# Perceiver block on one core: key chunks drawn over a block boundary, and the state space's small matmuls in pairs

## The chip, the cores and the metric
One NeuronCore of one Trainium2 chip runs the whole program. The metric is the device time of one execution in microseconds (us). TensorE (PE) does the matmuls, VectorE (DVE), ScalarE (ACT) and GpSimd (POOL) the elementwise work, SyncE (SP) issues most DMAs. Every engine runs its own list of instructions in order; semaphores tie the lists together.

## The reference, cut to what matters
One transformer-like block on x (8 x 64 x 512), in float32, three parts with a residual each.

```python
# 1. cross attention: q from x, k and v from ctx (8 batches x 1601 keys), 32 query heads, 8 key heads, head size 128
q = rmsnorm(layernorm(x) @ Wq.T);  k = rmsnorm(ctx @ Wk.T);  v = ctx @ Wv.T
x = x + softmax(q @ k.T / sqrt(128)) @ v @ Wo.T
# 2. state space (Mamba-2 form): 64 heads of 64, 8 groups of state size 128, causal convolution of 4 taps
gate, hbc, dt = split(layernorm(x) @ Win)
xs, B, C = split(silu(conv(hbc)));  dt = softplus(dt + bias)
state = state * exp(-dt * A) + dt * xs outer B;  y = state . C + D * xs      # over 64 tokens
y = y * rsqrt(mean(y * y) per group + eps) * norm_weight * silu(gate)
x = x + y @ Wout
# 3. routed low-rank experts: 8 experts, rank 16, the best one per token
x = x + experts(x)
```

All large products are computed as three float16 matmuls: each operand is split into a high and a low half (high x high, high x low, low x high). ScalarE makes the high half, VectorE or GpSimd the low one.

## The kernel before, in words
The program is a chain of blocks: `queries`, `cross_attention`, `output_projection`, `state_space_and_experts`. A block begins on all engines together, once all have ended the one before.

`queries` (L910) makes the queries of 32 heads in 8 groups of 4 tiles. TensorE projects a tile into one of four PSUM banks `pQ`, and two tiles later (`LAG = 2`) turns the normed tile with four transposes into one of two banks `pR` (`turn`, L1059 on), from which ScalarE (`high`) and VectorE (`low`) make the two halves. `turn` of tile n waits for VectorE's low half of tile n - 2. In gaps the block also splits the key and value weights and the context of batch 0. After the loop TensorE has the last two `turn`s; SyncE stores the last group to DRAM and ends the block.

`cross_attention` (L51) works through 64 units (8 batches x 8 key heads). "Fills" (projections of keys, 4 chunks of 400 or 401 columns, and of values, tiles in pairs) go through three PSUM banks `pF`: fill n waits for `fill_lo >= n - 2`, that is, until VectorE has taken the low half of fill n - 3. Around the change:
- Ahead of the first unit TensorE does four key fills, three value fills, `squares(0, 0)` (norms of the keys, by ones columns) and `turn_squares(0, 0)`. ScalarE copies the squares (`gather_squares`), VectorE adds eps (`norms`), GpSimd raises to -1/2 (`power`), and with that VectorE can evict scores (`evacuate`). VectorE's 12 memsets of constants come first in its list; ScalarE, GpSimd and SyncE (mask loads, then query loads) wait for `consts >= 5`.
- A unit on TensorE: seven score pieces with key fills of the next unit between them, one value fill (`vals(0)`), the values of the unit before, the transposes of the maxima, the next unit's squares, the spreading of the maxima, `vals(1)`, `turn_squares`. VectorE evicts scores in seven pieces, takes the maximum (one instruction of 6 us), and then the low halves of key chunks 2 and 3 (`keys(2)`, `keys(3)`).

`state_space_and_experts` (L1452) works through 8 groups g, software-pipelined by a list written out by hand for each engine: `body(g)` for g = 0 to 6 and `last` for g = 7; `on(f, g, lag, ...)` calls f for group g - lag. Per group TensorE has ten input chunks (`input_chunk`, 12 matmuls each, round three banks `pI`), four output tiles (`out_tile`, 12 matmuls each, all in bank `pO`, so that each waits for VectorE's `accumulate` of the one before), and for each of four token tiles the small float32 pieces:
- `turn_x` (L1738, transposes into the X half of the two banks `ab`), read by VectorE's `times_dt`;
- `keys_by_queries` (L1749, into `cd`), read by `causal`;
- `decay` (L1707, into the D half of `ab`, of GpSimd's `ramp`), read by ScalarE's `exponentials`;
- `outputs` (L1724, into `cd`), needs VectorE's `masked` and `times_dt`, read by `skip_added`;
- `squares` (L1757, into `cd`).
A piece waits for the readers of what was begun in its banks (the `begun` counts). Large matmuls are all at L797, the helper `split3`. VectorE's and ScalarE's `split_B`, `split_A` and `split_C` make the halves of the gate columns, the other input columns and the output weights of a group; `gates` (ScalarE) evicts the first four input chunks, `taps` and `finish_conv` do the convolution of the other six.

Of the kernel before, what the change touches and what calls it, by code (L numbers as in the profile page):

```python
# [10 lines left out]
P = 128  # L11
BATCH, TOK, HID = 8, 64, 512
KEYS = 1601
# [37 lines left out]
def cross_attention(nc, ctxT, maskT, kv_parts, ctx_parts, q_hi, q_lo, q_stored, o_dram, out_proj, NB=BATCH):  # L51

    with ExitStack() as ctx:
# [52 lines left out]
        proj = sem("proj")  # L106
# [152 lines left out]
        def _(pe):  # L259
# [98 lines left out]
            for i in range(NCH):  # L358
                key_fill(i, i, 0, 0, 0, i)
            for f in range(3):  # L360
                value_fill(NCH + f, NCH + f, 0, 0, f)
            pe.wait_ge(consts, 5)
            pe.wait_ge(idt, 2)
            squares(0, 0)
            turn_squares(0, 0)

            def body(b, par):
                for s in range(U):
# [55 lines left out]
                    vals(1)  # L424
# [13 lines left out]
        def _(act):  # L438
# [109 lines left out]
        def _(dve):  # L548
            dve.memset(k_h[:, :, KEYS:KPAD], 0.0)
            dve.memset(k_l[:, :, KEYS:KPAD], 0.0)  # L550
            dve.memset(sq_h[:, KEYS:KPAD], 0.0)
            dve.memset(sq_l[:, KEYS:KPAD], 0.0)
            dve.memset(pick[:, :, :], 0.0).then_inc(consts, 1)
            dve.wait_ge(consts, 1)
            for j in range(4):
                dve.memset(pick[:, j, j:j + 1], 1.0)
            dve.memset(half[:, :], -0.5)
            dve.memset(lnb[:, :], P_LN)
            dve.memset(ones_h[:, :], 1.0).then_inc(consts, 1)
            dve.memset(mask[:, KT - 1, :], NEG).then_inc(consts, 1)  # L560
            dve.memset(v_h[:, :, KT - 1, :], 0.0).then_inc(consts, 1)
            dve.memset(v_l[:, :, KT - 1, :], 0.0).then_inc(consts, 1)

# [94 lines left out]
            for i in range(NCH):  # L658
                key_fill(i, i, 0, i)
            for f in range(3):  # L660
                value_fill(NCH + f, NCH + f, 0, f)
            dve.wait_ge(mask_in, 32)

            def body(b, par):
                last = is_last(b)
                for s in range(U):
# [13 lines left out]
                    norms(b, s)  # L680
# [49 lines left out]
        def _(pool):  # L730
# [15 lines left out]
            pool.wait_ge(consts, 5)  # L746
            for i in range(NCH):
                low_squares(i, 0, 0, i)

# [160 lines left out]
def queries(nc, x, wqT, norm_w, q_hi, q_lo, kvT, ctxT, kv_parts, ctx_parts, stored):  # L910
# [4 lines left out]
    with ExitStack() as ctx:  # L915
# [36 lines left out]
        pT = [ctx.enter_context(nc.psum_tensor(f"q_pT{i}", [P, 512], F32)) for i in range(2)]  # L952
        pQ = [ctx.enter_context(nc.psum_tensor(f"q_pQ{i}", [P, 512], F32)) for i in range(TT)]
# [102 lines left out]
        def _(pe):  # L1056
# [28 lines left out]
            for t in range(TT - LAG, TT):  # L1085
                turn(GR // 2 - 1, 1, t)
# [365 lines left out]
def state_space_and_experts(nc, start, winG, woutG, params, x1, raT, bwT, out):  # L1452

    with ExitStack() as ctx:
# [125 lines left out]
        def _(pool):  # L1580
# [29 lines left out]
            def body(g, par):  # L1610
                on(join_squares, g, 2, 3)
# [3 lines left out]
                on(low, g, 2, 3)  # L1615
                on(ramp, g, 0, 0)
                on(low, g, 1, 0)
                on(join_squares, g, 1, 0)
                on(ramp, g, 0, 1)
                on(join_squares, g, 1, 1)  # L1620
                on(low, g, 1, 1)
                on(join_squares, g, 1, 2)
                on(low, g, 1, 2)
            def last(g, par):

                ramp(g - 1, 2)
                join_squares(g - 2, 3)
                low(g - 2, 3)
                power(g - 2)
                join_squares(g - 1, 0)  # L1630
                low(g - 1, 0)
                join_squares(g - 1, 1)
                ramp(g - 1, 3)
                ramp(g, 0)
                join_squares(g - 1, 2)
                low(g - 1, 1)
                join_squares(g - 1, 3)
                ramp(g, 1)
                low(g - 1, 2)
# [19 lines left out]
        def _(pe):  # L1659
# [7 lines left out]
            def input_chunk(g, n):  # L1667
# [4 lines left out]
                if n == GCH:  # L1672
                    wait(pe, wA_lo, g + 1)
                if n >= 3 + GCH:
# [786 lines left out]
```

## Time and profile before

| | |
|---|---|
| median of 3 runs | 2343.58 us (2342.84 to 2344.61) |
| profiled execution | 2342.31 us, span 2340.3 us |
| mean granted TensorE clock | 0.992 of full speed |
| PE | 2285.0 us busy, 98% of the span |
| DVE | 1917.5 us, 82% |
| ACT | 1297.5 us, 55% |
| POOL | 1579.3 us, 67% |
| queries end, attention begins | 118.5 us |
| state space begins | 1928.5 us |

Busy time is the union of an engine's instructions. The engines overlap, so the shares don't add up; the work of an engine that nothing waits for costs nothing. Times in the rows below are us from the span's start.

### The profile page before, as it was taken

What the parts mean: (1) busy time and instruction counts of PE and PEld (TensorE: products, weight loads), DVE (VectorE), ACT (ScalarE), POOL (GpSimd) and SP (SyncE); (2) the same over time, 40 slices, a digit from 0 to 9 for tenths busy, and PEclk for the clock granted to TensorE, in tenths of its full rate; (3) what the DMA queues carried; (4) which work ended last, traced back from release to release, by engine and by line L of the source; (5) the groups of instructions that cost most, each with busy time, mean ns of one, the idle gap of its engine ahead of it and who ended that gap; (6) DMA issues with size and microseconds to landing.
All of it is one profiled execution on the core that took longest, in us unless ns stands there. A gap on an engine that the chain in (4) does not pass through costs nothing. (4 is left out here: it accounts for less than half of the span.)

```text
span 2340.3 us, 46521 instructions
## 1 busy us (share of the span) xinstructions
PE 2285.0 (98%) x19276; PEld 1647.7 (70%) x19276; DVE 1917.5 (82%) x2600; ACT 1297.5 (55%) x2091; POOL 1579.3 (67%) x1059
## 2 busy tenths in 40 slices
PE   8999999999999999999999999999999898999998
PEld 4567787777877778777787777877778444445544
DVE  7858888888888888888888888888879957888877
ACT  7845455554555545555455555555545536666664
POOL 0138888888878888888887888888888402344432
PEclk9999999999999999999999999999999998999999
DMA  8421100000100011001000110100001443212210
GB/s 290 126 53 29 29 23 26 27 28 24 29 26 23 29 27 34 18 26 28 27 26 26 31 28 18 34 26 10 12 26 59 146 149 108 82 64 82 91 46 19
DMA packets 101166, 117.54 MB, mean 50 GB/s; under 512 B 8286, under 2 KB 70878, under 8 KB 100958
## 3 DMA queue, kind: packets, MB, share of 16 engines
q1 hardware_dynamic: 98942, 107.25, 14.5%
q0 software_dynamic: 2016, 7.34, 1.2%
q8 instruction: 153, 2.51, 0.5%
q14 instruction: 55, 0.45, 0.1%
HBM read 96.74 MB, written 17.83 MB: 49 GB/s over the span
## 5 line engine op out<-in xcount | busy, mean ns | idle before, releaser
L176 POOL TENSOR_TENSOR p_l<-S,p_h 128x1792 f16<-128x1792 f32 x126 | 423.6, 3362 | 204.8 <-ACT p_h L483 204.8
L598 DVE SCALAR_TENSOR_TENSOR S<-pS,rk,mask 128x256 f32<-128x256 f32 x832 | 355.5, 478 | 131.7 <-PE pS L263 84.9
L263 PE MATMUL p_acc<-w_l,ctx_h 128*128 128x256 f16 (+1 forms) x1664 | 453.6, 273 | 0.0
L263 PE MATMUL p_acc<-w_h,ctx_l 128*128 128x256 f16 (+1 forms) x1664 | 453.6, 273 | 0.0
L263 PE MATMUL p_acc<-w_h,ctx_h 128*128 128x256 f16 (+1 forms) x1664 | 453.6, 273 | 0.0
L608 DVE TENSOR_REDUCE mx<-S 128x256 f32<-128x3328 f32 x63 | 376.6, 5979 | 2.2
L263 PE MATMUL p_acc<-ctx_h,w_h 128*128 128x400 f16 (+1 forms) x1024 | 341.5, 334 | 3.0 <-PEq L915 3.0
L263 PE MATMUL p_acc<-ctx_l,w_h 128*128 128x400 f16 (+1 forms) x1024 | 341.5, 334 | 0.0
L263 PE MATMUL p_acc<-ctx_h,w_l 128*128 128x400 f16 (+1 forms) x1024 | 340.7, 333 | 0.0
L465 ACT ACTIVATE v_h<-p_acc 128x512 f16<-128x512 f32 (+1 forms) x224 | 126.7, 566 | 376.2 <-PE p_acc L263 376.2
L645 DVE TENSOR_TENSOR S<-S,pO 128x1792 f32<-128x1792 f32 (+1 forms) x128 | 240.9, 1883 | 86.3 <-PE pO L333 86.3
L737 POOL TENSOR_TENSOR sq_l<-sq_f,sq_h 128x400 f16<-128x400 f32 (+1 forms) x256 | 242.5, 947 | 71.3 <-ACT sq_h L457 71.3
L263 PE MATMUL pS<-qh,k_h 128*128 128x256 f16 x832 | 226.6, 272 | 1.8 <-DVE S L598 1.8
L263 PE MATMUL pO<-p_h,v_h 128*128 128x256 f16 x832 | 226.8, 273 | 0.0
L263 PE MATMUL pO<-p_l,v_h 128*128 128x256 f16 x832 | 226.8, 273 | 0.0
L263 PE MATMUL pO<-p_h,v_l 128*128 128x256 f16 x832 | 226.8, 273 | 0.0
L263 PE MATMUL pS<-qh,k_l 128*128 128x256 f16 x832 | 226.8, 273 | 0.0
L263 PE MATMUL pS<-ql,k_h 128*128 128x256 f16 x832 | 226.7, 272 | 0.0
L476 ACT ACTIVATE S<-S,lnb 128x1792 f32<-128x1792 f32 (+1 forms) x128 | 215.5, 1683 | 15.3 <-DVE S L645 15.3
L184 POOL TENSOR_TENSOR S<-S 128x1536 f32<-128x1536 f32 x63 | 216.8, 3441 | 0.1
L453 ACT ACTIVATE k_h<-p_acc 128x400 f16<-128x400 f32 (+1 forms) x256 | 129.6, 506 | 148.6 <-PE p_acc L263 146.6
L483 ACT ACTIVATE p_h<-S 128x1792 f16<-128x1792 f32 (+1 forms) x128 | 203.7, 1591 | 0.3
(285 smaller groups left out, 5221.9 us busy)
## 6 DMA issues: line engine op xcount, KB each, us to landing
ctx_p<-ctxT_dram SPq DMA_DIRECT2D x42, 458.0 KB, 3.6
s_wst<-winG_dram SPq DMA_DIRECT2D x8, 1536.0 KB, 6.5
q_wst<-wqT_dram SPq DMA_DIRECT2D x8, 1024.0 KB, 6.5
o_scratch<-o_st SPq DMA_DIRECT2D x32, 256.0 KB, 2.4
s_wst<-winG_dram SPq DMA_DIRECT2D x8, 1024.0 KB, 5.3
m_wost<-woutG_dram SPq DMA_DIRECT2D x8, 1024.0 KB, 5.2
qh<-q_hi_scratch SPq DMA_DIRECT2D x64, 64.0 KB, 1.9
ql<-q_lo_scratch SPq DMA_DIRECT2D x64, 64.0 KB, 2.0
```

Source lines behind the costliest of these rows:

```text
L176: eng.tensor_tensor(p_l[:, s % 2, t0:t1, :], S[:, s % 2, t0:t1, :], p_h[:, s % 2, t0:t1, :], ALU.subtract).then_inc(pl_ok, 1)
L184: eng.tensor_tensor(T[:, 0:6, :], T[:, 0:6, :], T[:, 6:12, :], ALU.add).then_inc(sum_ok, 1)
L263: mm = pe.matmul(out, x, y, start=first and j == 0, stop=final and j == 2)
L453: act.activation(k_h[:, head % 2, c0:c0 + w], bank[:, 0:w], ACT.Copy, scale=S_KV / (S_CTX * S_W))
L465: act.activation(v_h[0:m, job % 2, 2 * f:2 * f + tiles, :], pF[at % 3][0:m, 0:256 * tiles].rearrange("p (t c) -> p t c", c=256), ACT.Copy, ...
L476: act.activation(S[:, s % 2, t0:t1, :], S[:, s % 2, t0:t1, :], ACT.Exp, bias=lnb[:, 0:1]).then_inc(ph_ok, 1)
L483: act.activation(p_h[:, s % 2, t0:t1, :], S[:, s % 2, t0:t1, :], ACT.Copy).then_inc(ph_ok, 1)
L598: ins = dve.scalar_tensor_tensor(out=S[:, s % 2, t, :].rearrange("p (r q) -> p r q", r=REP), in0=bank[:, t % 2, :].rearrange("p (r q) -> p ...
L608: dve.tensor_reduce(mx[:, :], S[:, s % 2, :, :].rearrange("p t q -> p q t"), AX.X, ALU.max).then_inc(mx_ok, 1)
L645: dve.tensor_tensor(v, v, pO[s % 2][:, 1, :].unsqueeze(1).to_broadcast([P, t1 - t0, QC]), ALU.subtract).then_inc(sub_ok, 1)
L737: pool.tensor_tensor(sq_l[:, c0:c0 + w], sq_f[:, c0:c0 + w], sq_h[:, c0:c0 + w], ALU.subtract).then_inc(sql_ok, 1)
```

## The change
Two things. In `queries` and `cross_attention`: the four banks of the output projection (`fills`) are now shared by `queries`, the semaphore `proj` lives in both blocks, and the first two key fills of unit 0 are issued by TensorE at the end of `queries`, each behind one of the last two `turn`s. `cross_attention` starts with fill 2; squares and their transpose are put between the value fills, VectorE makes its constants behind two key chunks, and in the first unit `vals(1)` stands ahead of `turn_maxima`. In the state space: all four hand-written lists are reordered, and output tile 1 of groups 0 to 5 goes to bank `pI[1]`, with the waits for it.

```diff
 queries, TensorE
-            for t in range(TT - LAG, TT):
-                turn(GR // 2 - 1, 1, t)
+            def first_keys(i):
+                c0, w = CH[i]
+                wait(pe, kv_lo, 1)
+                wait(pe, ctx_lo, i + 1)
+                for k in range(KC):
+                    mm = split3(pe, fills[i][:, 0:w], (kv_h[:, 0, k, 0:HD], kv_l[:, 0, k, 0:HD]),
+                                (ctx_h[:, k, c0:c0 + w], ctx_l[:, k, c0:c0 + w]), k == 0, k == KC - 1)
+                mm.then_inc(proj, 1)
+            for i in range(AHEAD):
+                turn(GR // 2 - 1, 1, TT - LAG + i)
+                first_keys(i)
 cross_attention, TensorE ahead of the units
-            for i in range(NCH):
+            for i in range(AHEAD, NCH):
                 key_fill(i, i, 0, 0, 0, i)
-            for f in range(3):
-                value_fill(NCH + f, NCH + f, 0, 0, f)
+            value_fill(NCH, NCH, 0, 0, 0)
             pe.wait_ge(consts, 5)
             pe.wait_ge(idt, 2)
             squares(0, 0)
+            value_fill(NCH + 1, NCH + 1, 0, 0, 1)
             turn_squares(0, 0)
+            value_fill(NCH + 2, NCH + 2, 0, 0, 2)
 in a unit
                     if earlier:
                         values(*earlier, 0)
+                    else:
+                        vals(1)
                     if ahead:
                         turn_maxima(b, s)
 ...
                     spread_maxima(b, s)
-                    vals(1)
+                    if earlier:
+                        vals(1)
 ScalarE
-            act.wait_ge(consts, 5)
             for i in range(NCH):
                 key_fill(i, i, 0, 0, i)
-            for f in range(3):
+            value_fill(NCH, NCH, 0, 0, 0)
+            gather_squares(0, 0)
+            act.wait_ge(consts, 5)
+            for f in range(1, 3):
                 value_fill(NCH + f, NCH + f, 0, 0, f)
-            gather_squares(0, 0)
 VectorE (the memsets were the first thing in its list; norms(0, 0) was in the first unit)
-            for i in range(NCH):
+            key_fill(0, 0, 0, 0)
+            key_fill(1, 1, 0, 1)
+            constants()
+            for i in range(2, NCH):
                 key_fill(i, i, 0, i)
-            for f in range(3):
+            value_fill(NCH, NCH, 0, 0)
+            norms(0, 0)
+            for f in range(1, 3):
                 value_fill(NCH + f, NCH + f, 0, f)
 state space, waits on TensorE
+                if n == 1:
+                    wait(pe, acc, TT * (g - 1) + 2)
 ...
                 if bank is pO:
-                    wait(pe, acc, TT * (g + 1) + t)
+                    wait(pe, acc, TT * (g + 1) + (1 if t == 2 and g < L - 1 else t))
+                elif g < L:
+                    wait(pe, conv, CONV * (g + 1) + GCH)
 TensorE's body, as it was and as it is
-  input_chunk 0 | turn_x(g-1,3) | out_tile(g-2,3) | decay(g-1,3) outputs(g-1,2) | input_chunk 1, 2 |
-  squares(g-1,0) keys_by_queries(g-1,3) | input_chunk 3 | decay(g,0) outputs(g-1,3) | input_chunk 4 to 7 |
-  squares(g-1,1) | input_chunk 8, 9 | squares(g-1,2) squares(g-1,3) turn_x(g,0) | out_tile(g-1,0) |
-  keys_by_queries(g,0) turn_x(g,1) keys_by_queries(g,1) decay(g,1) | out_tile(g-1,1) |
-  decay(g,2) outputs(g,0) | out_tile(g-1,2) | keys_by_queries(g,2) turn_x(g,2) outputs(g,1)
+  input_chunk 0 | turn_x(g-1,2) keys_by_queries(g-1,1) | out_tile(g-2,3) | decay(g-1,2) outputs(g-1,1) |
+  input_chunk 1 | squares(g-1,0) turn_x(g-1,3) keys_by_queries(g-1,2) | input_chunk 2 |
+  decay(g-1,3) outputs(g-1,2) | input_chunk 3 | squares(g-1,1) keys_by_queries(g-1,3) | input_chunk 4 |
+  decay(g,0) outputs(g-1,3) | input_chunk 5 to 9 | squares(g-1,2) squares(g-1,3) turn_x(g,0) |
+  out_tile(g-1,0) | out_tile(g-1,1) in pI[1] | turn_x(g,1) keys_by_queries(g,0) | out_tile(g-1,2) |
+  decay(g,1) outputs(g,0)
 VectorE's body begins
-  split_B(g), accumulate(g-2,1), skip_added(g-1,0), masked(g-1,1), causal(g-1,2), gated(g-1,0), ...
+  split_B(g), times_dt(g-1,1), causal(g-1,0), masked(g-1,0), accumulate(g-2,1), accumulate(g-2,2),
+  skip_added(g-1,0), gated(g-1,0), times_dt(g-1,2), causal(g-1,1), masked(g-1,1), split_A(g), ...
 and ends (before)  taps(g,5), times_dt(g,0), accumulate(g-1,0), causal(g,0), times_dt(g,1), causal(g,1), masked(g,0)
 and ends (now)     taps(g,5), times_dt(g,0), accumulate(g-1,0)
```

ScalarE's list has both splits before the second exponentials, then square and high half of each tile in turn, and the gates in two runs of two; `split_C` on VectorE is cut in two halves; GpSimd joins the squares and makes the low half of a tile right after each other. `last` follows the same order up to input chunk 5.

## Rows read from the trace of the kernel before

**Rows 1.** Windows: start:end and length, busy us (instructions) by engine, granted clock, DMA.
```profile
118.50:124.40 5.90, 5.87 (x19) 2.66 (x20) 1.72 (x16) 1.29 (x3) 0.65 (x3) 0.51 0.96 238
160.00:200.00 40.00, 40.00 (x344) 31.41 (x342) 31.84 (x47) 25.56 (x36) 30.23 (x18) 1.00 0.10 27
2060.93:2107.57 46.64, 45.72 (x386) 23.45 (x386) 38.90 (x61) 31.52 (x41) 18.81 (x18) 1.00 0.24 80
```
**Rows 2.** Timeline of TensorE at the seam: start, duration, instruction, idle before it.
```profile
111.52 1.04 PE L1066 MATMUL q_pR<-q_ident,q_qs 128*128 128x128 f32 x8
114.93 0.63 PE L1066 MATMUL q_pR<-q_ident,q_qs 128*128 128x128 f32 x4 [2.38 <-DVE q_ql L1177]
118.53 0.49 PE L263 MATMUL p_acc<-ctx_h,w_h 128*128 128x400 f16 x1 [2.97 <-PEq L915]
...
127.42 0.33 PE L263 MATMUL p_acc<-ctx_h,w_h 128*128 128x401 f16 x1
...
129.46 0.27 PE L263 MATMUL p_acc<-w_h,ctx_h 128*128 128x256 f16 x1
```
**Rows 3.** Timeline of SyncE's DMA queue, the last issue of the queries' block.
```profile
117.51 0.58 SPq L1008 DMA_DIRECT2D q_lo_scratch<-q_ql  x1
```
**Rows 4.** Timeline of TensorE, its waits in the first unit of the attention.
```profile
138.40 0.33 PE L318 MATMUL p_acc<-ident,zr 128*128 128x128 f32 x1 [0.37 <-ACT zr L471]
...
142.54 0.28 PE L263 MATMUL pS<-qh,k_h 128*128 128x256 f16 x1 [0.47 <-DVE S L598]
...
156.33 0.44 PE L326 MATMUL pO<-ident,mx 128*128 128x128 f32 x2 [1.82 <-DVE mx L608]
```
**Rows 5.** Timeline of VectorE, low halves of key chunks 2 and 3 behind the maximum.
```profile
156.18 1.06 DVE L573 SCALAR_TENSOR_TENSOR k_l<-p_acc,k_h 128x400 f16<-128x400 f32 x2
```
**Rows 6.** Timeline of TensorE, four stops of a steady state-space group.
```profile
2100.45 0.38 PE L797 MATMUL m_b<-m_woh,m_yl 128*128 128x512 f16 x1
2101.24 0.45 PE L1749 MATMUL m_cd<-m_bc 128*64 128x64 f32 x8 [0.41 <-ACT m_bc L1955]
2101.62 0.66 PE L1738 MATMUL m_ab<-s_ident,m_xq 128*128 128x128 f32 x4
2102.21 0.45 PE L1749 MATMUL m_cd<-m_bc 128*64 128x64 f32 x8
2103.16 0.66 PE L1707 MATMUL m_ab<-m_R,s_after 64*64 64x256 f32 x8 [0.49 <-DVE m_dtx L2179]
2103.75 0.39 PE L797 MATMUL m_b<-m_woh,m_yh 128*128 128x512 f16 x1
...
2106.14 0.38 PE L797 MATMUL m_b<-m_woh,m_yl 128*128 128x512 f16 x1
...
2107.51 0.39 PE L797 MATMUL m_b<-m_woh,m_yh 128*128 128x512 f16 x1
...
2109.89 0.38 PE L797 MATMUL m_b<-m_woh,m_yl 128*128 128x512 f16 x1
...
2111.88 0.39 PE L797 MATMUL m_b<-s_th,s_wh 128*128 128x512 f16 x1
...
2114.26 0.38 PE L797 MATMUL m_b<-s_th,s_wl 128*128 128x512 f16 x1
...
2114.91 0.38 PE L797 MATMUL m_b<-m_woh,m_yh 128*128 128x512 f16 x1
```
**Rows 7.** Timeline of ScalarE, its split of the gate columns.
```profile
2101.09 1.90 ACT L1925 ACTIVATE s_wh<-s_wst 128x2048 f16<-128x2048 f32 x1
```
**Rows 8.** Timeline of VectorE, from the second product to its split of the gate columns.
```profile
2102.32 0.69 DVE L2179 TENSOR_TENSOR m_dtx<-m_ab,m_dtq 128x512 f32<-128x512 f32 x1 [0.29 <-PE m_ab L1738]
...
2103.72 2.29 DVE L2120 SCALAR_TENSOR_TENSOR s_wl<-s_wst,s_wh 128x2048 f16<-128x2048 f32 x1
```
**Rows 9.** Timeline of GpSimd, two ramps.
```profile
2103.92 2.99 POOL L1585 TENSOR_TENSOR m_R<-m_upto,m_a 128x512 f32<-128x512 f32 x1 [4.83 <-PE m_ab L1707]
...
2108.00 1.04 POOL L1585 TENSOR_TENSOR m_R<-m_upto,m_a 128x512 f32<-128x512 f32 x1
```

More of the change, by code:

```diff
@@ L548, in _ @@
         def _(dve):
[L549 to L562, printed above, removed]
             def ctx_split(b, par, n):
@@ L656, in output, with constants @@
                                          op0=ALU.mult, op1=ALU.mult).then_inc(o_ok, 1)
-            for i in range(NCH):
+            def constants():
+                dve.memset(k_h[:, :, KEYS:KPAD], 0.0)
+                dve.memset(k_l[:, :, KEYS:KPAD], 0.0)
+                dve.memset(sq_h[:, KEYS:KPAD], 0.0)
+                dve.memset(sq_l[:, KEYS:KPAD], 0.0)
+                dve.memset(pick[:, :, :], 0.0).then_inc(consts, 1)
+                dve.wait_ge(consts, 1)
+                for j in range(4):
+                    dve.memset(pick[:, j, j:j + 1], 1.0)
+                dve.memset(half[:, :], -0.5)
+                dve.memset(lnb[:, :], P_LN)
+                dve.memset(ones_h[:, :], 1.0).then_inc(consts, 1)
+                dve.memset(mask[:, KT - 1, :], NEG).then_inc(consts, 1)
+                dve.memset(v_h[:, :, KT - 1, :], 0.0).then_inc(consts, 1)
+                dve.memset(v_l[:, :, KT - 1, :], 0.0).then_inc(consts, 1)
+            key_fill(0, 0, 0, 0)
+            key_fill(1, 1, 0, 1)
+            constants()
+            for i in range(2, NCH):
                 key_fill(i, i, 0, i)
-            for f in range(3):
+            value_fill(NCH, NCH, 0, 0)
+            norms(0, 0)
+            for f in range(1, 3):
                 value_fill(NCH + f, NCH + f, 0, f)
@@ L678, in vals_earlier @@
                             value_fill(FILLS * eb + slot(es, NCH + i), slot(es, NCH + i), job, f)
-                    norms(b, s)
+                    if earlier:
+                        norms(b, s)
                     vals_earlier(0)
@@ L907, in identity, with queries @@
                        pattern=[[-1, P]], channel_multiplier=1).then_inc(sem, 1)
-def queries(nc, x, wqT, norm_w, q_hi, q_lo, kvT, ctxT, kv_parts, ctx_parts, stored):
+def queries(nc, x, wqT, norm_w, q_hi, q_lo, kvT, ctxT, kv_parts, ctx_parts, stored, fills, proj):
     with ExitStack() as ctx:
@@ L951, in queries @@
         ql = sb("q_ql", [P, 2, BATCH, 4 * TOK], F16)
-        pT = [ctx.enter_context(nc.psum_tensor(f"q_pT{i}", [P, 512], F32)) for i in range(2)]
-        pQ = [ctx.enter_context(nc.psum_tensor(f"q_pQ{i}", [P, 512], F32)) for i in range(TT)]
+        pT = fills[0:2]
+        pQ = fills[2:4] + [ctx.enter_context(nc.psum_tensor(f"q_pQ{i}", [P, 512], F32)) for i in range(2, TT)]
         pR = [ctx.enter_context(nc.psum_tensor(f"q_pR{i}", [P, 512], F32)) for i in range(2)]
@@ L2019, in body @@
                 on(first_tap, g, 0, 2)
+                on(high, g, 1, 3)
                 on(finish_conv, g, 0, 1)
@@ L2346, in last @@
                 tile_mean_square(g, 0)
-                split_C(g, par)
+                split_C(g, par, range(GCH))
                 skip_added(g, 1)
```

199 lines of the change are left out of this document (100 added, 99 removed).

## The prediction
> **What bounds the kernel now.** I read the windows first, then TensorE's own order of instructions, then the engines that feed it. In the attention TensorE has no idle time (40.00 us busy of 40); in a steady group of the state space it is busy 45.72 of 46.64 us, with VectorE at 38.90, ScalarE at 31.52 and GpSimd at 18.81 [rows 1]. So a change pays only where it shortens TensorE's own list or fills one of its few holes. The reader is to look at two places. One is the seam between the queries and the attention, where TensorE stands still and then runs at half clock. The other is what lies between two runs of large state-space matmuls (168 a group, one each 0.216 us): the stops for small matmuls, waits included.
>
> **The seam.** The last query chunk runs straight into two sets of transposes, from 111.52; the last set runs at 114.93, after 2.38 us of waiting for the low half of an earlier tile; then nothing until the attention's block opens at 118.53 [rows 2]. SyncE's last store issue ends at 118.09 [rows 3], so that one sets the opening, and the change leaves it alone. From 118.50 to 124.40 the granted clock is 0.51, the 1.2 GHz level, behind 6 us in which the engine did next to nothing; in the later stretch it is 1.00, 2.4 GHz [rows 1].
> The change puts key chunk 0 between those transposes and key chunk 1 behind them. A chunk at the full clock takes 129.46 - 127.42 = 2.04 us [rows 2]. Chunk 0 runs from about 112.6 to 114.6, before the 114.93 at which the next transposes could start anyway; chunk 1 from 115.6 to 117.6, before 118.09. Both are free.
> (1) Before, the four chunks take from 118.53 to 129.46, 10.93 us. Afterwards two stand behind the opening, 4.1 us if the clock holds: 6.9 us gained. I take it to hold, since TensorE's holes shrink from 2.4 and 3.0 us to about 0.3 and 0.9. Bounds: if the clock falls all the same, 5.9 us of matmuls behind the opening run at half rate and 2.95 us of the 6.9 are lost; nothing in the list can gain more than 6.9.
> (2) VectorE's and GpSimd's work behind the three value fills is drawn between them. Before, TensorE waits 0.37 us for ScalarE's copy of the squared norms, and 0.47 us at 142.54 for score evictions that start late because GpSimd's power comes late [rows 4]. In the new order norms and power run under the third value fill (24 matmuls, 2.6 us), so both waits go: 0.8 us; bounds 0 and 0.84.
> What could be late there: the constants stand behind two key chunks on VectorE, about 3 us later than now, and SyncE's mask loads and behind them the query loads wait for them. The first scores come at 118.5 + 4.1 + 3 x 2.6 + 0.8 = 131.2 and I see these loads landed by 129; if not, the mask holds VectorE for a microsecond. The value fill into bank 1 needs VectorE's low half of chunk 1, ready about 121.7, wanted at 122.6.
> (3) In the first unit the second value fill now goes ahead of the transposes of the maxima, into a hole of 1.82 us [rows 4]. I give it nothing. The fill reuses one of three banks and waits for the low half of key chunk 2 of this unit, which VectorE does only behind that same maximum. So the hole stays and gets longer by this low half: two of them take 1.06 us [rows 5], so 0.5 us is lost; bounds -1.0 and, if I misread the order, +1.8.
> Sum at the seam: 6.9 + 0.8 - 0.5 = 7.2 us.
>
> **The state space.** No large matmul is added or removed, so I price stops. In one group, with the last large matmul's 0.216 us taken off [rows 6]:
> - keys, transposes, keys, decay: 2100.45 to 2103.75, 3.08 us, of which 0.41 waits for ScalarE's last convolution, 0.49 for VectorE's product, and about 0.2 for the first keys' eviction.
> - decay, outputs: 2106.14 to 2107.51, 1.15 us.
> - keys, transposes, outputs: 2109.89 to 2111.88, 1.77 us.
> - transposes alone: 2114.26 to 2114.91, 0.43 us.
> The other stops of a group (squares, and the rest of decay with outputs) cost the same in both orders. The new order turns the first, third and fourth of these into three pairs of transposes and keys and one more pair of decay and outputs; no two pieces of a pair write one bank, so neither waits for VectorE to have read the other's. Transposes and keys as a pair are not in the trace. Keys take 0.38 where nothing holds the next piece (2101.24 to 2101.62), so the pair can't be under 0.43 + 0.38 = 0.81; from above, transposes to keys at 0.59 (2101.62 to 2102.21) with keys at 0.38 behind gives 0.97, and some tenths for a drain 1.07. I take 0.90, nearer the unhindered row. So before 3.08 + 1.77 + 0.43 = 5.28, after 3 x 0.90 + 1.15 = 3.85: 1.43 us a group, bounds 0.9 and 1.7. The period goes from 46.64 to 45.2.
> Are the waits really covered? I set the end of output tile 0 (2100.45 + 0.22) at 0. ScalarE's split of the gate columns starts at 0.42 and takes 1.90 [rows 7]; VectorE's half of it (2.29) follows, and now stands ahead of the second product, the causal product and the first masked product, which take 1.40 in all (2102.32 to 2103.72) [rows 8]. The split ends at 4.6, the product at 5.3, the masked one at 6.0. TensorE goes through tile 1, a pair and tile 2 (2.59 + 0.90 + 2.59) and reaches the second decay at 6.1, which needs the product, and the outputs about 6.6, which need the masked one: 0.6 us to spare, the tightest place, and the whole next group is queued behind it. The second output tile, now in input bank 1, finds its convolution done; the next chunk 1 into that bank comes at 14.4, and the accumulation that frees it ends near 6.7. The gate that frees bank 0 for chunk 3 now stands behind VectorE's other split and ScalarE's second high half; by the same durations it ends at 20, wanted at 21.7. The convolutions follow their input chunks by about 1 us, as before.
> Five intervals between steady groups and the last group, taken as one more, give 6 x 1.43 = 8.6. The step from group 0 to group 1 has no output tiles to cover anything and pays latency in either order; I take 0.5 us for it, bounds one group's gain either way.
> Sum: 9.1 us, bounds 6 x 0.9 - 1.4 = 4.0 and 6 x 1.7 + 1.4 = 11.6.
>
> **Total.** 7.2 + 9.1 = 16.3 us. The profiled execution has a span of 2340.3 and takes 2342.31; it would take 2326.0. The median of the runs is 1.27 us above it, so the forecast is 2327.3.
>
> **Rivals.**
> A. The clock falls at the seam all the same. For it: TensorE still pauses twice around the opening. Against it: 4 of the 6 quiet microseconds are filled. Price 2.95: 2330.2. The Trainium skill ("TensorE: Matmul & The Clock Gate", Part 1, What's actually happening) says that a restart costs a stretch of time and not a number of matmuls; by that rule the two chunks that leave the half-clock stretch would only be replaced in it by those that follow, and the result is this rival's. The trace shows one such stretch here and can't yet tell.
> B. The state space gains nothing, because a covered wait comes back elsewhere. For it: the 0.6 us above. Against it: VectorE keeps 6 us free in a group. Only the seam is left: 2336.4.
> C. Slower than before. One mechanism: VectorE's split of the gate columns, now ahead of the three products, meets GpSimd's ramp, and both stretch. The ramp takes 2.99 us beside that split and 1.04 elsewhere [rows 9]. The outputs wait from the point at which that chain is 0.6 us late, and each microsecond beyond is paid in 7 groups. To eat 7.2 and 9.1 it would have to be 0.6 + 16.3/7 = 2.9 us late in each; at 4 us late the time is 2343.6 - 16.3 + 7 x 3.4 = 2351.1. Against it: the split is at 2.29 with the ramp already beside it, so the stretch falls on GpSimd, which has time. The Trainium skill ("GPSIMD Engine Reference", 1. Specifications) says that GpSimd shares its SBUF interfaces with VectorE, with contention when VectorE's instruction has two SBUF inputs; by it a new order can add such meetings. The ramp's two durations agree.
> D. The pair costs 0.81 and the step out of group 0 gains as a full group: 6 x 1.7 + 1.4, so 2.5 more: 2324.8.
>
> **Chances.** Forecast as told 0.50, A 0.17, B 0.13, D 0.13, C 0.04, and 0.03 for no change by some mix of these. Range 2321.5 to 2337.5: it holds A, B and D with a microsecond or three of margin. What a measurement of this kernel can't tell from no change is 0.2%, 4.7 us. Faster by more than that 0.92, within it 0.04, slower 0.04.
>
> **What would show it.** At the seam: key matmuls between 112.6 and 117.6, the attention's first matmul still at 118.5, a granted clock near 1 from there to 124, first scores near 131.2, and a TensorE wait of about 2.4 us ahead of the first unit's second value fill. In the state space: a period of 45.2, transposes and keys at 0.90, no wait of the decay for VectorE and none of the keys for ScalarE. A period of 46.6 with new TensorE waits for the masked product would make B or C right; an opening of the block later than 118.5 would break the seam's sum.

## The result and the profile after

| | before | changed |
|---|---|---|
| median (range) | 2344.10 us (2342.64 to 2345.77, 6 runs) | 2327.75 us (2326.76 to 2329.58, 6 runs) |
| profiled execution, span | 2342.31, 2340.3 us | 2328.39, 2326.0 us |
| mean granted clock | 0.992 | 0.994 |

The ratio is 0.9929, with a 95% interval of 0.9919 to 0.9939: faster by 16.4 us. The forecast was 2327.3.

To see where the time went I cut the two profiled executions at the same instructions: the start of the last query matmul, the first scores of the first and of the second attention unit, the first matmul of the state space, the end of each group's last input chunk, and the end of the span.

| stretch, us | before | changed | difference | forecast |
|---|---|---|---|---|
| last query matmul to first scores | 27.26 | 19.92 | -7.34 | -7.3 |
| first scores to the second unit's | 22.05 | 21.58 | -0.47 | 0.0 |
| from there to the state space | 1767.94 | 1767.94 | 0 | 0 |
| its start to group 0's last chunk | 30.23 | 30.19 | 0 | 0 |
| step from group 0 to 1 | 45.18 | 45.57 | +0.4 | -0.5 |
| five steady groups | 5 x 46.64 | 5 x 45.30 | -6.7 | -7.2 |
| step from group 6 to 7 | 49.28 | 47.60 | -1.68 | -1.4 |
| from there to the end | 53.86 | 55.35 | +1.49 | 0 |

Windows of the changed kernel (start:end and length, then busy us and instructions by engine, granted clock, DMA), answering to [rows 1]: queries' end, the attention's opening, a steady group, and a stop near the end with what follows it.
```profile
112.44:118.58 6.14, 4.85 (x31) 2.66 (x28) 2.94 (x5) 2.63 (x9) 0.04 (x1) 1.00 0.54 156
118.58:124.40 5.82, 5.82 (x41) 3.90 (x42) 3.21 (x19) 4.95 (x12) 3.46 (x6) 1.00 0.58 162
1996.55:2041.85 45.30, 45.30 (x386) 23.52 (x385) 39.62 (x62) 32.07 (x40) 16.81 (x17) 1.00 0.25 82
2270.65:2274.55 3.90, 1.74 (x15) 1.24 (x14) 2.68 (x5) 3.66 (x4) 2.03 (x2) 0.88 0.01 2
2274.55:2277.10 2.55, 2.55 (x8) 0.90 (x7) 1.53 (x3) 2.43 (x4) 0.00 (x0) 0.51 0.00 0
```
The opening runs 41 matmuls at a granted clock of 1.00 where 19 ran at 0.51 [rows 1]. The group is 1.34 us shorter, and TensorE has no idle time left in it. Near the end the clock falls, which the kernel before doesn't show in its 3.49 us stop at this place:
```profile
2286.44:2289.93 3.49, 1.33 (x15) 0.88 (x14) 2.27 (x5) 3.24 (x4) 2.03 (x2) 1.00 0.01 2
2289.93:2292.50 2.57, 2.57 (x14) 1.08 (x11) 1.95 (x3) 2.46 (x4) 0.00 (x0) 1.00 0.00 0
```
TensorE at the seam in the changed kernel, answering to [rows 2] (start, duration, instruction, idle before it and its releaser):
```profile
111.56 1.04 PE L1080 MATMUL q_pR<-q_ident,q_qs 128*128 128x128 f32 x8
112.44 0.33 PE L811 MATMUL p_acc<-ctx_h,w_h 128*128 128x400 f16 x1
...
114.98 0.63 PE L1080 MATMUL q_pR<-q_ident,q_qs 128*128 128x128 f32 x4 [0.35 <-DVE q_ql L1203]
115.44 0.33 PE L811 MATMUL p_acc<-ctx_h,w_h 128*128 128x400 f16 x1
...
117.31 0.33 PE L811 MATMUL p_acc<-ctx_h,w_l 128*128 128x400 f16 x1
118.58 0.33 PE L265 MATMUL p_acc<-ctx_h,w_h 128*128 128x400 f16 x1 [0.94 <-PEq L929]
...
148.75 0.28 PE L265 MATMUL p_acc<-w_h,ctx_h 128*128 128x256 f16 x1 [2.31 <-DVE k_l L565]
```
Both chunks lie in the old holes, and the opening hasn't moved. The last row is the first unit's second value fill, waiting for the low half of key chunk 2. Neither wait of 0.37 nor of 0.47 [rows 4] is in the trace any more.

A steady group's stops in the changed kernel, answering to [rows 6]. Between the rows run large matmuls, 12 or 24 at a time; L1767 turns, L1778 are the keys, L1736 the decay, L1753 the outputs, L1786 the squares:
```profile
2047.86 0.60 PE L1767 MATMUL m_ab<-s_ident,m_xq 128*128 128x128 f32 x4
2048.39 0.45 PE L1778 MATMUL m_cd<-m_bc 128*64 128x64 f32 x8
2051.47 0.66 PE L1736 MATMUL m_ab<-m_R,s_after 64*64 64x256 f32 x8
2051.95 0.64 PE L1753 MATMUL m_cd<-m_E,m_dtx 64*64 64x64 f32 x32
...
2062.40 0.28 PE L1786 MATMUL m_cd<-s_ones,m_sqb 128*128 128x1 f32 x2
2062.54 0.64 PE L1767 MATMUL m_ab<-s_ident,m_xq 128*128 128x128 f32 x4
2063.10 0.45 PE L1778 MATMUL m_cd<-m_bc 128*64 128x64 f32 x8
```
No row has a wait. From the end of the last large matmul to the start of the next, the pair is 0.91 us twice and 1.09 with the squares in it; decay and outputs stay at 1.15.

### The profile page after: what moved, and what is told of

Its sections match the earlier page's. It is cut to its first block and busy times, and to the rows that moved or that the text cites. A ratio compares the mean times of both kernels' runs of the same rounds, so it can differ in the third digit from the quotient of the medians.

```text
span 2326.0 us, 46522 instructions
## 1 busy us (share of the span) xinstructions
PE 2278.8 (98%) x19276; PEld 1646.9 (71%) x19276; DVE 1920.4 (83%) x2600; ACT 1301.6 (56%) x2091; POOL 1569.2 (67%) x1059
## 3 DMA queue, kind: packets, MB, share of 16 engines
q0 software_dynamic: 2016, 7.34, 1.2%
## 5 line engine op out<-in xcount | busy, mean ns | idle before, releaser
L265 PE MATMUL p_acc<-ctx_h,w_h 128*128 128x400 f16 x1016 | 337.6, 332 | 0.9 <-PEq L929 0.9
L265 PE MATMUL p_acc<-ctx_l,w_h 128*128 128x400 f16 x1016 | 337.6, 332 | 0.0
L265 PE MATMUL p_acc<-ctx_h,w_l 128*128 128x400 f16 x1016 | 336.9, 332 | 0.0
```

The costliest lines, as they stand in the source:

```text
L265: mm = pe.matmul(out, x, y, start=first and j == 0, stop=final and j == 2)
```

## The experiments
Twelve kernels, each timed in five rounds (state_only has seven times). A ratio is against the kernel before on the same chip, whose medians there were 2344.1 to 2345.3 us, so medians of different rows can differ by about a microsecond for the chip alone. The columns are stretches of one profiled execution, as in the table above: A last query matmul to the second unit's first scores, B step 0 to 1, C one steady group, D step 6 to 7 and the rest to the end.

| kernel | median | ratio (interval) | A | B | C | D |
|---|---|---|---|---|---|---|
| before | 2344.10 | | 49.31 | 45.18 | 46.64 | 103.14 |
| changed | 2327.75 | 0.9929 (0.9919, 0.9939) | 41.50 | 45.57 | 45.30 | 102.95 |
| both_again | 2329.05 | 0.9930 (0.9917, 0.9944) | 41.51 | 45.61 | 45.30 | 103.01 |
| seam_only | 2335.65 | 0.9958 (0.9944, 0.9971) | 41.49 | 45.23 | 46.64 | 103.13 |
| state_only | 2337.84 | 0.9970 (0.9958, 0.9981) | 49.13 | 45.74 | 45.30 | 103.02 |
| low_first | 2328.13 | 0.9931 (0.9917, 0.9944) | 39.45 | 45.60 | 45.30 | 102.93 |
| products_first | 2330.22 | 0.9940 (0.9927, 0.9954) | 41.50 | 44.49 | 45.77 | 101.72 |
| one_chunk_ahead | 2335.23 | 0.9958 (0.9945, 0.9972) | 46.52 | 45.57 | 45.30 | 102.99 |
| tile1_shared_bank | 2354.54 | 1.0041 (1.0028, 1.0055) | 43.02 | 45.54 | 50.5 or 48.8 | 105.16 |
| keys_before_turn | 2328.10 | 0.9931 (0.9917, 0.9944) | 41.49 | 46.18 | 45.38 | 101.47 |
| tail_decay | 2329.06 | 0.9930 (0.9917, 0.9944) | 41.50 | 45.72 | 45.30 | 102.81 |
| fill_back | 2328.90 | 0.9935 (0.9922, 0.9949) | 41.21 | 45.74 | 45.30 | 103.02 |
| assembled | 2325.06 | 0.9917 (0.9903, 0.9930) | 39.42 | 44.45 | 45.30 | 101.50 |
| squares_early | 2325.64 | 0.9919 (0.9905, 0.9932) | 39.43 | 44.28 | 45.30 | 100.13 |

**The parts alone.** both_again is the changed kernel once more. seam_only takes all of its text but the state space's function, state_only that function alone.

> The changed kernel as it is, beside its parts on one chip. Theory (gains at the seam and in the state space add up): 16 us below the kernel before. Rival (the 2 us by which the profiled executions differ from the medians are a gain of its own, of some executions): the profiled span would be 2 us lower than 2326.0 here.

> Only the first part of the change: the two key chunks in the queries' block and the reordered beginning of the attention; the state space as before. Theory: 7.8 us below the kernel before, all of it by the first scores of the second unit (152.9 for 160.6 in the traces). Rival (the state space hides part of it): under 6 us.

> Only the second part: the four reordered lists and output tile 1 in its own bank; queries and attention as before. Theory: five groups at 1.34 us each, nothing in the first step and little in the last group: 6.5 to 7 us below the kernel before. Rival (the last group gains like the others and the profiled execution only missed it for its clock): 8 to 8.5 us.

The medians move by 9.7 us for the seam and 7.5 for the state space, 16.3 for both against the same runs of before: they add within a microsecond. Columns A and C show each part gone without touching the other; seam_only's gain in A is 7.82 us, the 7.8 expected, and the medians are too uncertain to tell it from 9.7 (its interval is 6.8 to 13.1 us). The loss in B and the fall of the clock in D come with the state space's part.

**The low half ahead of the maximum** (low_first), VectorE in a unit:
```diff
+                    if not earlier:
+                        keys(2)
                     (maximum of the scores)
-                    keys(2)
+                    if earlier:
+                        keys(2)
```


> The changed kernel with one edit: in the first unit VectorE takes the low half of key chunk 2 ahead of the maximum instead of behind it. Theory (the second value fill in TensorE's hole waits for that low half, as its 2.31 us at 148.75 shows): the fill runs at once under the maximum, the maximum comes 0.5 us later, and TensorE's wait shrinks from 2.3 to under 0.5 us: 1.8 to 2 us faster than the changed kernel. Rival (the fill waits for ScalarE or for the bank's reader of another fill): no change.

A falls by 2.05 us, and TensorE's 2.31 us becomes
```profile
150.66 0.44 PE L328 MATMUL pO<-ident,mx 128*128 128x128 f32 x2 [0.21 <-DVE mx L600]
```
So the wait was VectorE's order and not its load. The medians (2328.13 against 2329.05 of both_again) are too near each other to show it; the stretch does.

**The second value fill back in its old place** (fill_back):
```diff
-                    else:
-                        vals(1)
...
-                    if earlier:
-                        vals(1)
+                    vals(1)
```


> The changed kernel with the second value fill of the first unit back behind the spread over the partitions, where it was before; all else as changed. It tests the prediction's term (3), that moving the fill ahead of its neighbours costs 0.5 us since it waits for the low half of key chunk 2. Theory of the prediction: from first scores to the second unit's first scores 21.58 us goes back to 21.1, and the time falls by 0.5 us against the changed kernel. Rival: the hole it filled (1.8 us, waiting for VectorE's maximum) opens again and costs as much as the fill's wait did (2.31 us); the stretch stays within 0.2 us of 21.6.

First scores to the second unit's take 21.29 us, 0.29 less than in the changed kernel. Both waits of the kernel before (1.82 and 0.30 us) are back:
```profile
148.30 0.44 PE L328 MATMUL pO<-ident,mx 128*128 128x128 f32 x2 [1.83 <-DVE mx L597]
149.60 0.43 PE L335 MATMUL pO<-ident,top 128*128 128x128 f32 x2 [0.30 <-DVE top L626]
```
Together 2.13 us, where the changed kernel waits 2.31. The move costs something, as term (3) said, but 0.29 and not 0.5: besides the 1.8 us hole the fill covers a second one of 0.30. (The waits differ by 0.18; the other 0.11 us I can't place.) The median can't tell 0.3 us.

**One key chunk ahead instead of two** (one_chunk_ahead): `AHEAD = 1`, both turns as before.

> The changed kernel with only key chunk 0 in the queries' block; chunk 1 comes back behind the opening, so TensorE stands still for 3 us ahead of it. Theory (the clock held at the seam because both holes were filled): it falls again, 2.0 us for the chunk and up to 3 us for the half clock, 4 to 5 us slower than the changed kernel. Rival (one chunk is activity enough): the clock stays at 1.00 and it is 2.0 us slower.

A is 5.02 us longer, as expected, but put together otherwise. The hole at the opening and what runs behind it:
```profile
117.46:120.44 2.98, 0.01 (x1) 0.03 (x1) 0.75 (x1) 0.71 (x2) 0.04 (x1) 0.90 0.18 53
120.44:123.40 2.96, 2.96 (x10) 1.40 (x11) 0.57 (x1) 1.27 (x3) 1.40 (x3) 0.53 0.99 285
```
The opening to the first scores takes 16.09 us instead of 12.69: 2.04 for the chunk and 1.36 for the clock. The other 1.62 us come 30 us later: behind the wait of 2.31 us ahead of the second value fill the clock is 0.50 from 154 to 156, in the changed kernel 1.00 behind the same wait. The number was right for A, half of its reason wrong. The whole profiled execution is 6.9 us longer than the changed kernel's, and 1.9 of it are lost ahead of the last query matmul, where the code is the same; the median is 7.5 us higher, with times from 2330.5 to 2338.6.

**VectorE's products ahead of its split** (products_first), in all groups:
```diff
-                on(split_B, g, 0)
                 on(times_dt, g, 1, 1)
                 on(causal, g, 1, 0)
                 on(masked, g, 1, 0)
+                on(split_B, g, 0)
```


> The changed kernel with VectorE's split of the gate columns moved behind the second product, the causal and the first masked product, in every group. Theory (in steady groups that chain is covered by output tiles; only the step from group 0 to group 1 has none, and there the second decay waits 3.82 us for a product that stands behind the split): the step gets 2 to 2.5 us shorter, the period of 45.30 stays. Rival C of the prediction (the split ahead of the products costs in every group, hidden in the 45.30): the period falls below 45.3. Other rival (the split later holds the next input chunk): the step gains nothing.

It tests what the step from group 0 to 1 waits for. In the changed kernel, TensorE and then VectorE:
```profile
1954.96 0.63 PE L1767 MATMUL m_ab<-s_ident,m_xq 128*128 128x128 f32 x4 [3.39 <-ACT m_bc L1987]
1955.52 0.45 PE L1778 MATMUL m_cd<-m_bc 128*64 128x64 f32 x8
1959.79 1.13 PE L1736 MATMUL m_ab<-m_R,s_after 64*64 64x256 f32 x8 [3.82 <-DVE m_dtx L2207]
```
```profile
1956.75 2.29 DVE L2147 SCALAR_TENSOR_TENSOR s_wl<-s_wst,s_wh 128x2048 f16<-128x2048 f32 x1 [1.90 <-ACT s_wh L1957]
1958.96 0.69 DVE L2207 TENSOR_TENSOR m_dtx<-m_ab,m_dtq 128x512 f32<-128x512 f32 x1
```
The decay waits for a product that stands behind the split, and the split waits for ScalarE. In the kernel with the products first:
```profile
1957.10 1.13 PE L1736 MATMUL m_ab<-m_R,s_after 64*64 64x256 f32 x8 [0.49 <-DVE m_dtx L2207]
1960.20 0.61 PE L811 MATMUL m_b<-s_th,s_wh 128*128 128x512 f16 x1 [1.07 <-DVE s_wl L2147]
```
3.82 has become 0.49, but only 1.08 us are gained: the next group's first chunk now waits for the split. In the steady groups the later split delays what VectorE does next, until TensorE waits for it. VectorE:
```profile
2056.76 1.65 DVE L2222 TENSOR_TENSOR m_E<-m_Ec,m_cbm 128x512 f32<-128x512 f32 x1
2061.60 1.11 DVE L2231 SCALAR_TENSOR_TENSOR m_yt<-m_xq,m_par,m_cd 128x128 f32<-128x128 f32 x4
```
In the changed kernel these two stand at 2056.75 with 0.78 us and at 2060.72, and the group before them ends within 0.02 us of the same time in both. With the split behind the products, GpSimd's low half of a tile starts at 2056.70 instead of 2055.82 and meets the masked product, which takes 0.87 us more (the last section has more of such meetings). So the reading of the outputs (the second row) ends at 2062.71, and the sums of squares, which write that bank, follow at 2062.81:
```profile
2062.20 0.38 PE L811 MATMUL m_b<-s_th,s_wl 128*128 128x512 f16 x1
2062.81 0.35 PE L1786 MATMUL m_cd<-s_ones,m_sqb 128*128 128x1 f32 x2 [0.24 <-issue]
...
2063.98 0.39 PE L811 MATMUL m_b<-s_th,s_wh 128*128 128x512 f16 x1
```
1.56 us instead of 1.09: 0.47 per group, which is all of the difference in column C. Of this kernel's orders the changed one is right for the steady groups and wrong for the first step.

**Tile 1 back in the shared bank** (tile1_shared_bank): the output tile and its accumulation use `pO` in all groups.

> The changed kernel with output tile 1 back in the one bank of the others. Theory (the new order rests on that bank: tile 2 would have to wait for VectorE's accumulation of tile 1, which now stands behind the split and three products and ends 6.7 us after tile 0, where tile 2 wants to start at 3.5): 3.2 us for each of 6 groups, 19 us slower than the changed kernel, slower than the kernel before. Rival (only the direct wait between tiles 0 and 1): 1 us a group, 6 us.

Two waits for the accumulation in each group, 19.8 us in all by the view of waits:
```profile
2055.63 0.38 PE L811 MATMUL m_b<-m_woh,m_yh 128*128 128x512 f16 x1 [1.10 <-DVE x L2258]
...
2061.40 0.38 PE L811 MATMUL m_b<-m_woh,m_yh 128*128 128x512 f16 x1 [2.21 <-DVE x L2258]
```
The groups of 50.5 us have a stretch at a low clock behind this stop (0.68 from 2061 to 2065 in one), those of 48.8 have none; the fall is worth 1.7. The clock also takes 1.5 us of column A, behind the 2.30 us wait ahead of the second value fill. The median is 26.8 us above the changed kernel's, where 19 was expected. Without any fall a group takes 3.5 us more, 21 in six groups; the rest is the clock, and 2.5 us lost ahead of the last query matmul, in code that is the same. The second bank isn't a detail of this order: without it the order is slower than the kernel before.

**Keys ahead of the transposes in a pair** (keys_before_turn).

> The changed kernel with the two pieces of three pairs swapped: keys ahead of transposes. They still share no bank. Theory (the price of a pair hangs on which piece stands last; keys then transposes cost 1.09 in the last group of the kernel before, transposes then keys 0.91 now): 0.18 us for each of three pairs in 6 groups, 3 us slower than the changed kernel, period 45.8. Rival (a pair without a common bank costs the same both ways round): no change, period 45.3.

```profile
2048.51 0.38 PE L811 MATMUL m_b<-m_woh,m_yl 128*128 128x512 f16 x1
2048.82 0.45 PE L1778 MATMUL m_cd<-m_bc 128*64 128x64 f32 x8
2049.20 0.66 PE L1767 MATMUL m_ab<-s_ident,m_xq 128*128 128x128 f32 x4
2049.70 0.38 PE L811 MATMUL m_b<-m_woh,m_yh 128*128 128x512 f16 x1
```
The last large matmul ends at 2048.51 + 0.22 = 2048.73, so the stop is 0.97 us against 0.91. The group is 0.08 longer, not the 0.5 expected. (In the step from group 0 to 1, where nothing covers it, 0.6 is lost; the end gains 1.5, for the clock holds there.) The order within a pair hardly matters: the rival was right. What the pairs save is what stood between the pieces before, waits of 0.41 and 0.49 us among it [rows 6]; no run changes that alone.

**The last group's first decay one place earlier** (tail_decay), in `last`; ScalarE's exponentials go with it:
```diff
                 input_chunk(g, 4)
+                decay(g, 0)
                 outputs(g - 1, 3)
...
                 squares(g - 1, 3)
-                decay(g, 0)
                 turn_x(g, 0)
```


> The changed kernel, with the last group's first decay product taken out of the stop behind the last input chunk. It is issued before the outputs of the group before, behind input chunk 4, as the loop's body does it, and ScalarE's exponentials of it stand behind the first convolution tap. Theory: in the changed kernel that stop is 3.90 us: 0.2 for sums of squares, 0.47 for the decay product, 2.16 of wait for ScalarE's exponentials and the transposes. The wait goes, the product costs about 0.5 us at its new place, and the clock, which falls to 0.50 behind the stop and takes 1.2 us from the output tile, stays up. So from the last input chunk to the end it takes 55.4 - 2.2 - 1.2 = 52.0 us, and the time is 3.4 us under the changed kernel's. Rival: the work behind it hangs on the chain of VectorE and GpSimd (the 7.9 us stop before the last tiles), not on TensorE; then only the start of that stop moves, and the time is within 1 us of the changed kernel's. A third possibility: the stop's length shrinks but the clock falls at another stop of the end; gain about 2.2 us.

The theory failed. The stop shrinks from 3.90 only to 2.84 us, because a second chain ends 2.69 us behind the last input chunk, in the changed kernel as here. TensorE and VectorE in it:
```profile
2272.05 0.63 PE L1767 MATMUL m_ab<-s_ident,m_xq 128*128 128x128 f32 x4
2274.76 0.59 PE L811 MATMUL m_b<-m_woh,m_yh 128*128 128x512 f16 x1 [2.08 <-DVE x L2258]
```
```profile
2272.52 0.15 DVE L2251 TENSOR_SCALAR m_rsm<-m_cd 128x4 f32<-128x4 f32 x1
2273.86 0.75 DVE L2258 SCALAR_TENSOR_TENSOR x<-m_b,m_rs,x 128x512 f32<-128x512 f32 x1 [1.19 <-issue]
```
Output tile 1 needs the bank that this accumulation empties. The accumulation needs the mean square and its power by GpSimd (1.02 us, the idle 1.19 in the last row), and both need the sums of squares, which TensorE does last and ends at 2272.19. VectorE's own order holds the mean square a little longer, behind convolutions that end at 2272.60. The clock falls all the same, the product costs 0.43 us at its new place, and D gains 0.14 us.

**All three orders together** (assembled): low_first, tail_decay, and the products ahead of the split in group 1 alone.

> The changed kernel with three orders taken from the other runs: the low half of key chunk 2 is made ahead of the maximum in the first unit (2.06 us gained in its own run), VectorE splits the second group's B weights behind its three products, in that group alone (1.08 us in the step from group 0 to 1), and the last group's first decay product stands in the group before (up to 3.4 us). If they add, the time is 6.5 us under the changed kernel's, about 2321.5 us on its profile. Rival: if the end hangs on VectorE and GpSimd, 3.1 us under it, about 2325 us.

Against the changed kernel it gains 2.08 us in A, 1.12 in B and 1.45 in D, and the span goes from 2326.0 to 2321.5. That is not the 6.5 us expected. Nor is D's gain the order's, which gave 0.14 in tail_decay: the other 1.3 us come from the next stop, of 7.44 us. Behind it TensorE runs at half clock here as in the kernels before, changed and tail_decay, but for a shorter time. From the last group's last decay product to the sums of squares that wait 1.29 us, 11.8 us pass here, 13.25 in tail_decay with the same code, and 13.1 to 13.3 in the kernels before and changed. So 3.2 us are the orders' and 1.3 are luck. All five times (2323.84 to 2325.91) are below all five of fill_back (2328.74 to 2330.05) on the same chip; one of tail_decay's five, 2323.46, is lower still. It has the lowest median here, though its interval overlaps the changed kernel's.

**The sums of squares earlier too** (squares_early): assembled, and in `last`
```diff
                 squares(g - 1, 2)
+                squares(g - 1, 3)
                 input_chunk(g, 7)
...
                 taps(g, 2)
+                mean_square(g - 1)
                 taps(g, 3)
                 taps(g, 4)
-                mean_square(g - 1)
```


> The assembled kernel with one more order in the last group: TensorE's sums of squares for tile 3 of the group before stand two input chunks and more earlier, beside those of tile 2 ahead of input chunk 7, and VectorE's mean square, which needs them, stands behind its third convolution instead of its fifth. Theory: with the decay product gone, the stop behind the last input chunk is 2.84 us in the assembled kernel because of a chain that starts there (sums of squares, VectorE's mean square 0.15, GpSimd's power of it 1.02, VectorE's accumulate 0.75, which frees the bank of output tile 1). GpSimd had the squares joined 12 us before. Started early, the accumulate ends with the transposes: the stop shrinks from 2.84 to about 0.8 us, and the clock, which falls to 0.50 behind it and costs 1.2 us more, stays at 1.00. From the last input chunk to the end it takes 53.48 - 2.0 - 1.2 = 50.2 us, and the time is about 2321.8 us. Rival: the next stop, 7.44 us with 2.8 us of waits for VectorE, GpSimd and ScalarE in it, takes back what comes earlier; then the gain is 1.2 us (the clock) or less, and the time 2324 us or more.

The chain was the right one. The stop in this kernel, and the tile behind it:
```profile
2271.42:2272.91 1.49, 0.59 (x5) 0.38 (x4) 1.49 (x3) 1.29 (x2) 0.00 (x0) 1.00 0.02 5
2272.91:2275.51 2.60, 2.60 (x12) 1.08 (x12) 2.53 (x4) 0.52 (x1) 0.00 (x0) 1.00 0.00 0
```
1.49 us and not 0.8, because the accumulation stands behind a convolution that ends at 2272.1; the clock stays up, and the output tile behind it takes 2.60 us. The edit moves both the squares and VectorE's mean square, so it doesn't tell which of the two held the chain. Up to the next stop this gains 2.8 us (1.35 in the stop, 1.68 behind it, less 0.23 in the step from group 6 to 7), near the 3.2 expected. But D gains only 1.37: the 1.4 us that assembled had saved in the half-clock stretch behind the next stop are back. The two kernels there, assembled first:
```profile
2290.00:2295.00 5.00, 5.00 (x51) 2.52 (x49) 4.26 (x8) 2.63 (x4) 2.70 (x3) 0.79 0.01 3
```
```profile
2290.00:2295.00 5.00, 5.00 (x15) 2.14 (x15) 4.57 (x9) 2.63 (x4) 2.42 (x2) 0.50 0.01 3
```
The median doesn't move, and the profiled execution is 1.8 us longer than assembled's: besides those 1.4 us it loses 2.95 at 1851 and 0.75 ahead of the last query matmul, in code that is the same in both. That is the last section.

## Why the prediction was right
Its main mechanisms were right, and so was its time, the time in part by luck. In the trace the seam gives 7.8 us for 7.2 forecast and the state space 6.5 for 9.1, inside the bounds of 4.0 to 11.6. Two steps failed, the first step of the loop and the end.

- **Seam, term (1), 6.9 us.** Right, clock included. To the first scores 7.34 us went where (1) and the 0.37 wait make 7.27. one_chunk_ahead shows that the second chunk is what holds the clock at the opening: with a hole of 2.98 us it falls.
- **Term (2), 0.8 us.** Right, both waits are gone. The second was worth more than its 0.47 us of idle time: in the kernel before, the score piece behind it starts 0.63 us later than in an unhindered row, and another one a little further on 0.12 later. That makes 0.75.
- **Term (3), -0.5 us.** Right in kind: the wait is there, at 2.31 us for "about 2.4", and the fill's move loses 0.29 in the pair changed and fill_back. What the forecast missed is the 0.30 us wait for the second reduction, which the fill also covers. The stretch then goes from 22.05 to 21.29 in fill_back, which is the 0.75 us of term (2), and back to 21.58.
- **A steady group, 1.43 us.** 1.34 measured. The pair was forecast at 0.90 and is 0.91; with the squares, which cost 0.13 alone, it takes 1.09 - 0.13 = 0.96. These three make 0.08 of the 0.09 missing.
- **The tightest place.** The masked product was to be 0.6 us early. It ends at 2050.81 + 0.69 = 2051.50 with the outputs at 2051.95: 0.45 us early, and no wait. VectorE's split ahead of it takes 2.29 us, as in [rows 8]. Rival C's meeting with GpSimd's ramp doesn't happen there.
- **Step from group 0 to 1, +0.5 us.** Wrong in sign: 0.4 us lost. The forecast said that nothing covers this step and then gave it a third of a group's gain. The measured wait is 3.82 us, for a product behind the split. The same order that is covered by two output tiles in a steady group (split ahead of the products) has nothing over it here; products_first gets 1.08 back.
- **The end, forecast unchanged.** Wrong by 1.49 us. The stop was there before (3.49 us, 2.16 of it waiting for ScalarE), but the forecast read no row of it. The changed kernel loses 1.6 us there, all to the clock: 0.4 in the stop, whose last transposes run at half rate, and 1.2 in the tile behind it (3.83 us for 2.60). It can come and go: of the nine kernels that have the new state space and this wait, three, each with a further edit, don't pay it (last section).
- **Rival A** lost at the seam, and the forecast's doubt about it was fair: what a fall costs is about half of the slow time in which TensorE works. That slow time is 5.9 us with 19 matmuls at the opening before [rows 1], 2.96 with 10 in one_chunk_ahead, 2.55 with 8 at the end of the changed kernel. The costs are 2.8 us (10.93 for four chunks of 2.04), 1.36 and 1.23. The Trainium skill ("TensorE: Matmul & The Clock Gate", Part 1, What's actually happening) says that a restart costs a stretch of time and not a number of matmuls. The trace agrees that there is no fixed number; the worked part of the stretch isn't fixed either, since some of it passes in waits.

That the total came out within 0.5 us is luck. The errors are -0.6 at the seam, +0.9 at the first step, +0.5 in the steady groups, -0.3 at the last step and +1.5 at the end. They cancel only in part, to +2.0 on the profiled execution (a span 14.3 us shorter for 16.3 forecast). The scatter of the executions hides the rest: the changed kernel's profiled one is 0.64 us above its median, that of before 1.8 below, where the forecast took 1.27.

## What to carry to other kernels
Price small matmuls between large ones by the stop they make, from last large to next large, and group them so that no piece waits for a reader of its neighbour's bank; here that was worth 1.34 us of 46.6, and only with a second bank for the output tile: the same order without it took 48.8 us a group. Price the first and the last step of a pipelined loop from their own rows, since an order that the steady groups cover stands bare there. When a stop ends on a wait, look for the waiter just behind it before you move anything: here removing 2.16 us left 2.08.

## What the runs showed of the hardware
**The same wait, with the clock held or not.** Four places show it. Each kernel was profiled in one execution:

- The end: 2.16 us idle for ScalarE. The clock stays at 1.00 in before, seam_only, products_first, keys_before_turn and tile1_shared_bank, and falls to 0.5 in the changed kernel, both_again, low_first, state_only, one_chunk_ahead and fill_back.
- The first unit: 2.30 or 2.31 us idle. The clock falls in one_chunk_ahead (1.62 us) and tile1_shared_bank (1.5), and holds in the changed kernel, both_again, seam_only, products_first, keys_before_turn and tail_decay.
- The end's next stop, about 7.5 us: the clock falls in assembled and tail_decay alike, but costs 1.3 us less in the first.
- The output projection's opening, 2.32 or 2.33 us idle. The clock holds in thirteen of the fourteen kernels. Windows of assembled and of squares_early, whose code is the same up to there:
```profile
1851.00:1855.00 4.00, 4.00 (x20) 1.82 (x19) 4.00 (x6) 0.70 (x1) 2.64 (x4) 1.00 1.01 316
```
```profile
1852.00:1856.00 4.00, 4.00 (x14) 1.50 (x13) 4.00 (x6) 1.56 (x2) 3.44 (x7) 0.65 0.82 263
```
One holds, the other pays 2.95 us from the second unit to the state space (1770.90 against 1767.95). Something besides the length of the stop decides; no run here isolates it. Nor do the runs tell whether it goes with the kernel or with the execution: the five times of tail_decay alone lie between 2323.46 and 2331.97 us. For this kernel it means that 1 to 3 us can come and go without the edit at hand having earned them, and that a gain of that size has to be looked for in its own stretch. Shortening the stop may help: in the one kernel that had it at 1.49 us the clock held.

**VectorE stretched by GpSimd.** The masked product takes 0.69 us alone and 1.67 beside GpSimd's low half:
```profile
2064.19 1.67 DVE L2222 TENSOR_TENSOR m_E<-m_Ec,m_cbm 128x512 f32<-128x512 f32 x1
```
```profile
2064.16 1.15 POOL L1629 TENSOR_TENSOR m_yl<-m_y,m_yh 128x512 f16<-128x512 f32 x1
```
The group of this product over five steady groups in the changed kernel (count, busy us and mean ns of one, idle before):
```profile
L2222 DVE TENSOR_TENSOR m_E<-m_Ec,m_cbm 128x512 f32<-128x512 f32 x20 | 24.2, 1208 | 1.8
```
Ten of the 20 take 1.67 to 1.69 us beside a low half, five 0.77 or 0.78 and five 0.69. Before, the mean is 740 ns, and the longest is 0.91, beside a ramp: the new order costs 0.47 us a product on average. In the changed kernel no TensorE wait comes of it. In products_first it does: there one such meeting stands ahead of the stop with the squares. This is the meeting that the prediction looked for at the split and the ramp, found elsewhere.
